# A graph network's edge phase: the first layer of two edge pairs placed between the pieces of a node product

## The reference

```python
src, dst = edge_index
edge_feat = concatenate([x[src], x[dst], edge_attr], axis=-1)   # 512 + 512 + 64
h = mish(edge_feat @ W1 + b1)                                   # first layer of an edge
messages = mish(h @ W2 + b2)                                    # second layer of an edge
agg = segment_sum(messages, dst, num_segments=N)                # the sums
u = mish(concatenate([x, agg], axis=-1) @ W3 + b3)              # W3: half for x, half for agg
out = u @ W4 + b4
return layernorm(x + out)
```

## Time and profile before

| what | value |
| --- | --- |
| median of 3 runs | 1177.58 us (1175.31 to 1177.83) |
| the profiled execution | 1177.56 us, of which the span from first to last instruction is 1175.8 us |
| PE busy | 1076.2 us, 92% of the span |
| ACT, DVE, POOL busy | 77%, 76%, 57% |
| mean granted clock of PE | 0.939 of 2.4 GHz |

### The profile page before, as it was taken

One profiled execution on the slowest core, in us unless ns is written; L12 is line 12 of the kernel. 1 busy time (PEld: TensorE's weight loads), 2 busy tenths in 40 slices (PEclk: granted clock), 3 DMA queues, 4 the chain that ended last, 5 costly groups with the idle time before them and its releaser, 6 DMA issues.

```text
span 1175.8 us, 18391 instructions
## 1 busy us (share of the span) xinstructions
PE 1076.2 (92%) x5689; PEld 907.3 (77%) x5690; DVE 888.4 (76%) x1493; ACT 899.6 (77%) x1134; POOL 672.0 (57%) x564
## 2 busy tenths in 40 slices
PE   3566998899798889999999999999999999999897
PEld 0112888899587778888888888888888888888695
DVE  7798525453546148888898998989988888888787
ACT  6795843542520479999999999999999999999584
POOL 8696303000314267767788888888876776760117
PEclk7565998999799989999999999999999999999899
DMA  2001920120144367666666666666666666661002
GB/s 99 8 1 55 184 85 0 35 83 1 72 150 128 63 145 153 150 137 133 136 134 142 130 135 141 134 136 140 131 139 138 140 132 132 143 133 44 1 2 87
DMA packets 61087, 121.40 MB, mean 103 GB/s; under 512 B 7851, under 2 KB 18348, under 8 KB 60918
## 3 DMA queue, kind: packets, MB, share of 16 engines
q0 software_dynamic: 38048, 87.58, 36.8%
q1 hardware_dynamic: 22998, 33.32, 8.4%
HBM read 107.82 MB, written 7.80 MB: 98 GB/s over the span
## 4 chain that ended last, share of the span: by engine, by line
PE 83%; DVE 10%; ACT 3%; issue 2%; POOL 1%; DVEq 1%; ACTq 0%; POOLq 0%
PE banks L990 12%; PE banks L985 12%; PE banks L986 12%; PE banks L879 9%; PE banks L970 6%; PE banks L1005 6%; PE banks L964 6%; PE banks L941 5%; PE banks L805 4%; PE banks L922 4%; DVE edge_counts L1601 3%; PE banks L983 3%; DVE key_onehot L1557 2%; PE banks L1051 2%; PE banks L859 1%
## 5 line engine op out<-in xcount | busy, mean ns | idle before, releaser
L646 POOL DMA_INDIRECT gather_pq<-q_table,dst x157 | 299.0, 1904 | 61.9 <-issue 47.5
L638 POOL DMA_INDIRECT gather_pq<-p_table,src x157 | 173.3, 1104 | 159.1 <-PE banks L970 107.0
L985 PE MATMUL banks<-w_lo,h_hi 128*128 128x512 f32 x628 | 245.2, 390 | 0.0
L986 PE MATMUL banks<-w_hi,h_hi 128*128 128x512 f32 x628 | 244.9, 390 | 0.0
L990 PE MATMUL banks<-w_hi,h_lo 128*128 128x512 f32 x628 | 168.4, 390 | 0.0
L1863 DVE SCALAR_TENSOR_TENSOR h_full<-mish_work,banks 128x512 f32<-128x512 f32 (+1 forms) x158 | 100.9, 680 | 51.2 <-ACT mish_work L1274 48.5
L986 PEld LDWEIGHTS banks<-w_hi,h_hi 128*128 128x128 f32 x628 | 118.3, 188 | 25.3
L990 PEld LDWEIGHTS banks<-w_hi,h_lo 128*128 128x128 f32 x628 | 117.9, 188 | 24.5
L985 PEld LDWEIGHTS banks<-w_lo,h_hi 128*128 128x128 f32 x628 | 118.4, 189 | 22.2
L1262 ACT ACTIVATE mish_work<-banks 128x1024 f32<-128x1024 f32 (+1 forms) x79 | 80.6, 1021 | 31.4 <-PE banks L970 31.4
L964 PE MATMUL banks<-ident,gather_pq 128*128 128x128 f32 x628 | 95.8, 275 | 7.6 <-DVE h_full L1863 7.6
(11 more groups left out here) (249 smaller groups left out, 2723.9 us busy)
## 6 DMA issues: line engine op xcount, KB each, us to landing
edge_attr<-in_edge_attr_t SPq DMA_DIRECT2D x79, 128.0 KB
x_nodes<-h_hi POOLq DMA_DIRECT2D x10, 256.0 KB, 12.9
x_nodes<-h_lo POOLq DMA_DIRECT2D x10, 256.0 KB, 7.9
p_table<-p_stage SPq DMA_DIRECT2D x10, 256.0 KB, 2.0
q_table<-agg_nodes SPq DMA_DIRECT2D x10, 256.0 KB
gather_pq<-p_table,src POOLq DMA_INDIRECT x157
gather_pq<-q_table,dst POOLq DMA_INDIRECT x157
x_nodes<-in_x SPq DMA_DIRECT2D x3, 768.0 KB, 6.3
```

Source lines behind the costliest of these rows:

```text
L638: nc.gpsimd.indirect_dma_start(GP[:, 2 * j + k, :], None, p_tab[:, :], bass.IndirectOffsetOnAxis(ap=SRC[:, 2 * s + k:2 * s + k + 1], axis= ...
L646: nc.gpsimd.indirect_dma_start(GP[:, 2 * j + k, :], None, q_tab[:, :], bass.IndirectOffsetOnAxis(ap=DST[:, 2 * s + k:2 * s + k + 1], axis= ...
L985: pe.matmul(at, H_HI[:, j, c, e], W2_LO[:, c, :], start=False, stop=False)
L986: pe.matmul(at, H_HI[:, j, c, e], W2_HI[:, c, :], start=False, stop=False)
```

## The change

1. PE issues z1 of pair 0 behind piece 5 of the 16 and z1 of pair 1 behind piece 11 (`Z1_BEHIND = (5, 11)`). After the last piece comes the first tile of z2(0), and the edge steps start at s = 2.
2. ACT loads the exp/log table ahead of the copies of pieces, makes the attribute parts of pairs 0 and 1 there, then waits for the stored Q table, and puts mish of pairs 0 and 1, one activation behind each copy, between the copies; attributes of pairs 2 and 3 follow in the same way.
3. The results of those two pairs can't stand where `HT_HI` and `HT_LO` are still read. `EARLY_A` (mish work) and `EARLY_F` (`h_full`) of pairs 0 and 1, and `EARLY_HI` and `EARLY_LO` of pair 0, lie in the place of `AGG`, which is free once Q is stored. `h_hi` and `h_lo` of pair 1 go to their usual place, so `h_hi(1)` waits for all pieces.
4. DVE therefore zeroes `AGG` later: behind its step 2, after waits for `h_lo(1)` and for z2 of pair 0.

```diff
+Z1_BEHIND = (5, 11)
...
+        EARLY_A, at = sb("mish1_work_early", [P, KD, PW], at=agg_at)
+        EARLY_F, at = sb("h_full_early", [P, KD, PW], at=at)
+        EARLY_HI, at = sb("h_hi_early", [P, KD, PW], F32R, at=at)
+        EARLY_LO, at = sb("h_lo_early", [P, KD, PW], F32R, at=at)
+        assert at <= t1_at
+
+        def early(s, n):
+            return isinstance(s, int) and s < n
...
+                    u_terms(Z2[:, n % 4, 0:BW], W3A_HI, W3A_LO, HT_HI, HT_LO, o, b)
+                    if n in Z1_BEHIND:
+                        s = Z1_BEHIND.index(n)
+                        z1(s, s, s, 64)
+            z2(0, 0, 0)
+            for s in range(2, SLOTS):
                 edge_step(s, s, 64, None)
...
             nc.scalar.preload_act_table_set("natural_log_exp_and_others")
...
             for j in range(2):
                 attr_high(j, j, 16)
-            for s in range(2):
-                edge_step(s, s, 32)
+            act.wait_ge(q_stored, TABLE_STORED)
+            for b in range(BLOCKS):
+                for o in range(KD):
+                    n = KD * b + o
+                    act.wait_ge(mm_done, MM_UP + n + 1)
+                    if n == 12:
+                        act.wait_ge(rows_used, 2 * NT)
+                    nc.scalar.activation(u_part(b, o)[:, 0, :], Z2[:, n % 4, 0:BW], ACT.Identity, bias=COLS[:, CB3 + o:CB3 + o + 1]).then_inc(up_moved, 1)
+                    for s, first in enumerate(Z1_BEHIND):
+                        if n == first:
+                            exp1(s)
+                        if n == first + 1:
+                            sq1(s)
+                        if n == first + 2:
+                            log1(s)
+                        if n == first + 3:
+                            inv1(s)
+                        if n == first + 4:
+                            attr_high(s + 2, s, 32)
...
             def hi1(s, j):
...
+                if early(s, 2) and not early(s, 1):
+                    dve.wait_ge(mm_done, MM_U)
...
             dve.wait_ge(q_stored, TABLE_STORED)
+            for s in range(3):
+                edge_step(s, s % 2, s // 2)
+
+            dve.wait_ge(h_lo, 2)
+            dve.wait_ge(z2_done, 1)
             nc.vector.memset(AGG[:, :, :], 0.0).then_inc(agg_done, 1)
-            for s in range(4):
-                edge_step(s, s % 2, s // 2)
+            edge_step(3, 1, 1)
```

More of the change, by code:

```diff
@@ L282, in gnn_kernel, with z1_work, h_full_of, h_high @@
         assert at <= h1t_at + 4 * KH * NP
+        EARLY_A, at = sb("mish1_work_early", [P, KD, PW], at=agg_at)
[5 more added lines that the diff above has]
+            return isinstance(s, int) and s < n
+        def z1_work(s):
+            return EARLY_A if early(s, 2) else EA
+        def h_full_of(s):
+            return EARLY_F if early(s, 2) else HF
+        def h_high(s, j):
+            return EARLY_HI[:, :, :] if early(s, 1) else H_HI[:, j, :, :]
+        def h_low(s, j):
+            return EARLY_LO[:, :, :] if early(s, 1) else H_LO[:, j, :, :]
         AG_HI, _ = sb("agg_t_hi", [P, KD, NP], F32R, at=h1t_at + 4 * KD * NP)
@@ L943, in u_terms @@
                 mm.then_inc(mm_done, 1)
[L945 to L954, removed]
             def z1(s, slot, j, gathered):
@@ L984, in z2 @@
                 for c in range(KD):
-                    pe.matmul(at, H_HI[:, j, c, e], W2_LO[:, c, :], start=False, stop=False)
-                    pe.matmul(at, H_HI[:, j, c, e], W2_HI[:, c, :], start=False, stop=False)
+                    pe.matmul(at, h_high(s, j)[:, c, e], W2_LO[:, c, :], start=False, stop=False)
+                    pe.matmul(at, h_high(s, j)[:, c, e], W2_HI[:, c, :], start=False, stop=False)
                 if k == 0:
@@ L989, in z2 @@
                 for c in range(KD):
-                    mm = pe.matmul(at, H_LO[:, j, c, e], W2_HI[:, c, :], start=False, stop=(c == KD - 1))
+                    mm = pe.matmul(at, h_low(s, j)[:, c, e], W2_HI[:, c, :], start=False, stop=(c == KD - 1))
                 if k == tiles(s) - 1:
@@ L1027, in edge_step @@
                     extras1(more_tiles, s - 4)
-            for s in range(SLOTS):
+            pe.wait_ge(w3a_lo, 1)
+            pe.wait_ge(mm_moved, FREE + MM_PQ + NT)
+            for b in range(BLOCKS):
+                for o in range(KD):
+                    n = KD * b + o
+                    if n == 2:
+                        pe.wait_ge(q_moved, NT)
+                    if n >= 4:
+                        pe.wait_ge(up_moved, n - 3)
+                    u_terms(Z2[:, n % 4, 0:BW], W3A_HI, W3A_LO, HT_HI, HT_LO, o, b)
[4 more added lines that the diff above has]
+            for s in range(2, SLOTS):
                 edge_step(s, s, 64, None)
@@ L1246, in _ @@
             p_out(NT - 1)
[L1248 to L1254, removed]
             nc.scalar.preload_act_table_set("natural_log_exp_and_others")
@@ L1261, in exp1 @@
                     act.wait_ge(h_full[1], s)
-                nc.scalar.activation(EA[:, :, 0:P * tiles(s)], Z1v[:, :, 0:P * tiles(s)], ACT.Exp).then_inc(a_exp, 1)
+                nc.scalar.activation(z1_work(s)[:, :, 0:P * tiles(s)], Z1v[:, :, 0:P * tiles(s)], ACT.Exp).then_inc(a_exp, 1)
             def sq1(s):
                 act.wait_ge(a_exp, s + 1)
-                nc.scalar.activation(EA[:, :, 0:P * tiles(s)], EA[:, :, 0:P * tiles(s)], ACT.Square, bias=SQ_SCALE, scale=SQ_SCALE).then_inc(a_sq, 1)
+                nc.scalar.activation(z1_work(s)[:, :, 0:P * tiles(s)], z1_work(s)[:, :, 0:P * tiles(s)], ACT.Square, bias=SQ_SCALE, scale=SQ_SCALE).then_inc(a_sq, 1)
             def log1(s):
                 act.wait_ge(a_sq, s + 1)
-                nc.scalar.activation(EA[:, :, 0:P * tiles(s)], EA[:, :, 0:P * tiles(s)], ACT.Ln, bias=1.0, scale=SQ_BACK).then_inc(a_ln, 1)
+                nc.scalar.activation(z1_work(s)[:, :, 0:P * tiles(s)], z1_work(s)[:, :, 0:P * tiles(s)], ACT.Ln, bias=1.0, scale=SQ_BACK).then_inc(a_ln, 1)
             def inv1(s):
                 act.wait_ge(a_ln, s + 1)
-                nc.scalar.activation(EA[:, :, 0:P * tiles(s)], EA[:, :, 0:P * tiles(s)], ACT.Exp, scale=-1.0).then_inc(a_r, 1)
+                nc.scalar.activation(z1_work(s)[:, :, 0:P * tiles(s)], z1_work(s)[:, :, 0:P * tiles(s)], ACT.Exp, scale=-1.0).then_inc(a_r, 1)
             def z2_work(s):
@@ L1862, in full1 @@
                 at = (slice(2 * h, 2 * h + 2), slice(0, P * tiles(s)))
-                nc.vector.scalar_tensor_tensor(HF[:, at[0], at[1]], EA[:, at[0], at[1]], -0.5, Z1v[:, at[0], at[1]],
+                nc.vector.scalar_tensor_tensor(h_full_of(s)[:, at[0], at[1]], z1_work(s)[:, at[0], at[1]], -0.5, Z1v[:, at[0], at[1]],
                                                ALU.add, ALU.mult).then_inc(h_full[h], 1)
@@ L1870, in hi1 @@
                     dve.wait_ge(z2_done, s - 1)
-                nc.vector.tensor_copy(H_HI[:, j, :, 0:P * tiles(s)], HF[:, :, 0:P * tiles(s)]).then_inc(h_hi, 1)
+                if early(s, 2) and not early(s, 1):
+                    dve.wait_ge(mm_done, MM_U)
+                nc.vector.tensor_copy(h_high(s, j)[:, :, 0:P * tiles(s)], h_full_of(s)[:, :, 0:P * tiles(s)]).then_inc(h_hi, 1)
             def lo1(s, j):
                 dve.wait_ge(h_hi, s + 1)
-                nc.vector.tensor_tensor(H_LO[:, j, :, 0:P * tiles(s)], HF[:, :, 0:P * tiles(s)],
-                                        H_HI[:, j, :, 0:P * tiles(s)].bitcast(F32), ALU.subtract).then_inc(h_lo, 1)
+                nc.vector.tensor_tensor(h_low(s, j)[:, :, 0:P * tiles(s)], h_full_of(s)[:, :, 0:P * tiles(s)],
+                                        h_high(s, j)[:, :, 0:P * tiles(s)].bitcast(F32), ALU.subtract).then_inc(h_lo, 1)
             def hots1(s, j):
```

## The result

The changed kernel takes 1168.49 us in the median (1167.75 to 1170.21) against 1176.44 for the kernel before, run beside it: a ratio of 0.9936, 95% interval 0.992 to 0.9952, so 7.5 us faster (5.6 to 9.4; the two medians differ by 7.95). Run again beside later experiments it gave 0.9934 (0.9921 to 0.9947). The forecast was 1169.0 and −8.6 us. That 1169.0 lies only 0.5 from the measured median is in part luck: the forecast started from 1177.58, and the kernel before took 1.1 us less when it ran beside the changed one.

A forecast was written before the change was run, and what follows sets the result against it. PE was taken as full in the edge loop, so only the ramp before z1 of pair 5 could shrink: 438.4 plus 1.7 of clock gives 440.1 instead of 448.8, −8.6 us, 1169.0; 8-in-10 range 1166.4 to 1172.8.

The forecast's parts named there:

- The ramp: PE's stretch before z1 of pair 5, with idle gaps of 2.35, 5.19 and 2.21 us; z1(5) forecast 8.6 us earlier.
- both small stalls: PE waits 0.75 us before z2 of pair 0, for the last copy, and 0.25 us before z1(3).
- ACT's free wait for the Q table: ACT's wait ahead of the first copy ends at 378.06 instead of 376.83; with cover of 3.3 us it costs nothing.
- the free mish between the copies: Pair 0's mish on ACT takes 7 us instead of 4.3 between copies, costing PE and the copies nothing.
- The zeroing: On DVE between steps 2 and 3, 4.33 us; PE idles 3.2 us before z1(4), 2.75 of them the zeroing's.
- The clock: PE's 3.2 us gap before z1(4) draws the low clock, costing 1.7 us; rival without loss or smaller stall, chance 0.16.
- The gathers: Rival, chance 0.12: pair 0's gathers land late and stall z1 of pair 0, margin 0.4 us; 1170.0 at 1 us.
- Slower, or nothing: Two rivals, chance 0.04 each: the edge loop locks into a slower rhythm, 1181.4; something behind it sets the end, 1177.6.

The follow-up runs named there:

- e3: Kernel before with only the table load and the attribute parts of pairs 0 and 1 ahead of the copies, no interleaving, zeroing early: 1173.22 us, ratio 0.998.
- e7: Changed kernel with only pair 0's first layer between the pieces, pair 1's behind the last piece: 1172.34 us, ratio 0.9972 to the kernel before.
- e5: Changed kernel with the late zeroing written as five memsets of two tiles at the same place: 1169.42 us, one run.
- e2: Changed kernel with the zeroing cut in parts, only tiles 4 to 7 (2048 elements) left between DVE's steps 2 and 3: 1163.74 us, ratio 0.9893.
- e1: Changed kernel with the zeroing cut in three parts, all ahead of DVE's step 2: 1162.91 us, ratio 0.9889 to the kernel before.
- e4: Changed kernel with z1 of pair 0 behind piece 3 instead of piece 5: 1173.52 us, one run.

## Why the prediction was right

Dates from the first piece on, forecast (counted from 374.88) and measured (from 375.49):

| event | forecast | measured |
| --- | --- | --- |
| z1 of pair 0 | 10.56 | 10.56 |
| z1 of pair 1 | 23.0 | 22.93 |
| z2 of pair 0 | 32.7 | 32.58 |
| z1(2) | 35.67 | 35.67 |
| z1(3) | 43.8 | 43.62 |
| end of `h_lo(2)` on DVE | 49.6 | 49.41 |
| z1(4) | 54.8 | 55.35 |
| z1(5) | 65.3 | 65.67 |

**The ramp.** Its steps came as written, including both small stalls (0.75 forecast, 0.62 measured as idle and 0.78 by starts; 0.25 and some 0.2), ACT's free wait for the Q table and the free mish between the copies. e3 and e7 show what the parts bring in turn: 3.5, 1.5 and 3.2 of the 8.2.

**The zeroing.** Right in kind: it moved from free time onto the path, DVE holds `h_full(3)` and PE waits. The one term that was mis-sized is its length. I took the row's 4.33 and wrote that the trace disagreed with the page "VectorE: DVE Perf Modes" of the Trainium skill, whose rule of one cycle for each element made about 5.3. The runs side with the Trainium skill's page: 5.26 and 5.29 between neighbours (changed, e5), 3.23 for 3072 elements (e2). The held a hint that I passed over: 1.13 us of idle without a cause right before the memset. PE's gap was 3.8 instead of 3.2. Three smaller errors hid about half of this one: DVE was 0.2 earlier than I had it, z1(4) followed `h_full(3)` by 0.68 us instead of 0.84, and the clock cost 1.6 instead of 1.7. That the ramp came to −8.2 against −8.6 is luck to that extent.

**The clock.** 1.7 us forecast; mean grant 0.66 over 5 us in the changed kernel, and 1.5 to 1.6 us come back in e1 and e2 when the gap goes. What I gave for a reason was only a ranking of gap lengths, and e4 shows that it isn't the whole rule (below). Its gap of 3.15 us, as long as the 3.2 that I forecast, was followed by full clock, so that the low clock came as forecast is in part luck too. Behind the gap as it is, of 3.8 us, it came in all five traces that have one (the changed kernel twice, e4, e5, e7).

**The gathers.** The rival's place was real: there was a margin of 0.2 us in the first trace, and a wait of up to 0.24 in most others. It cost too little to decide.

**Slower, or nothing.** Two pairs take 17.32 us before and after, and the rest behind the ramp 727.0 and 727.2: the loop neither gave the gain back nor found a worse rhythm, also not with DVE late by the zeroing.

## What to carry to other kernels

When work is moved to fill a ramp, list what its new buffers push away: the zeroing, free before, cost 3.6 us of gap and 1.5 of clock, more than the 3.2 that pair 1's interleaving brought. Cut such a clearing by what lies in each part of the buffer and put each part where its own reader is done. And price an instruction by the distance between its neighbours' starts and ends, not by its row: an idle time without a releaser right before it may be the instruction itself, as it was for this zeroing.

## What the runs showed of the hardware

- A memset's row on DVE covers only part of the time that it takes from the engine: 0.91 of 1.07 us for 1024 elements, 4.33 of 5.3 for 5120 (e5, changed kernel). The rest stands as idle time ahead of the row.
- Two gathers of 128 rows, issued as the first of several, land some 3.7 us behind the end of the second one's issue: it ends at 381.45 in e4, and z1 of pair 0 is let go at 385.15.
- In and around the ramp the granted clock fell behind gaps of PE of 2.21 and 2.35 (before), 2.23 (e7), 2.24 (e3), 3.79 (e4, e7), 3.81 and 3.82 us (changed kernel, e5), and behind the 5.19 of e3. It didn't fall behind 0.59 (e2), 0.62 and 1.67, nor behind the 3.15 of e4, which is longer than the 2.2 that drew it elsewhere. And in 55 to 60 us of the changed kernel's trace the mean grant is 0.66 too, though the longest gap since 49 us is one of 1.50. Length alone doesn't decide; what else does wasn't tried and stays open.
